# Node numbers for the one-hots kept in PSUM and counted on by VectorE from step ten

## The chip, the cores and the metric

One Trainium2 chip, one of its cores. The metric is the device time of one execution in microseconds, the median of three runs.

## What is computed

One layer of a graph network over 6250 nodes of width 256 with 100,000 edges that are sorted by their target node. A graph convolution (gather, sum by target node, divide by degree) and a linear attention are added to the input; then a mixture of eight experts of width 1024 with a capacity works on the result.

```python
Wh = x @ W + b                         # _L0_gnn_ref, on the normalized x
summed = jax.ops.segment_sum(Wh[edge_src], edge_dst, num_segments=N_NODES)
deg = jax.ops.segment_sum(jnp.ones(...), edge_dst, num_segments=N_NODES)
h = summed / jnp.maximum(deg, 1.0)[:, None]
...
x = x + _L0_gnn_ref(xn, W, b, src, dst) + _L0_mix_ref(xn[None], ...)[0]
x = x + _L0_ffn_ref(_layernorm(x)[None], ...)[0]     # top-1 of 8 experts, capacity 977
```

## The kernel before

The nodes are cut into 49 tiles of 128 (`NT`). The segment sum of a tile is a matmul on TensorE: for each chunk of 128 edges, a one-hot matrix (edges by nodes) times the gathered rows. A one-hot is made by VectorE: it compares the 128 node numbers of the tile with the target of each edge (`is_equal`). Chunks go in groups of four (`G`), and gathered groups stand in a ring of seven (`RQ`).

**GpSimd (POOL)** gathers. `gather` issues four indirect DMAs per group (L614), each of which takes 128 row numbers from `idx` in SBUF; 196 groups make 784 such DMAs. Before every even group it looks whether a tile's results are due (`events`): if group f lies more than `LAG` = 5 past the last group of tile t+2, `event(t)` waits until VectorE has placed tile t (`row_ok`), scatters its rows (L564) and, from tile ten on, sends the rows of one finished expert job (`finish`, L551). Then it goes on gathering.

**VectorE** runs one `step` per tile: `late` (one-hots beyond the first four groups, L1462), `degrees` (L1564 counts the degree from PSUM, then L1573 to L1576), `early` for the next tile (L1488, four groups in one instruction of 128 x 2048), `combine`, `node_out`, `place` (ends with `row_at`, L1649, and `row_ok`), `plan`, `residual`, `route`, and `post` of an expert job. **TensorE** in a step does the projection of the last tile, one expert job (`expert`, `hidden`), the transposes, and then the sum of the next tile. **ScalarE** scales the sum (`ready`), normalizes a job's rows, takes a square root (`deviation`, L764), and does the hidden layer's ReLU (L799). SyncE loads weights and rows.

Steps 0 to 9 carry the attention (`pairs`); there the early one-hots are made in four parts (`early_part`). Steps from `T0` = 10 on carry expert jobs. After step 48 there are no sums left and the remaining expert jobs run.

The node numbers stand in `node_ids`, an SBUF tile of two halves: tile t uses half t % 2. In every step ScalarE adds 256 to the half of tile t (`count_on`, L732) behind `ready`, so that it serves tile t + 2, and VectorE waits for that (`nodes_ok`) inside `degrees`, behind L1564. `one_hot` and `early` read `node_ids` and `dst_t`, both in SBUF. The bank `pQ` holds the attention's queries up to step nine and nothing later.

## Time and profile before

| | us |
|---|---|
| median of three runs | 1847.22 |
| lowest, highest | 1834.12, 1854.69 |
| span of the profiled execution | 1845.7 |
| device time of the profiled execution | 1847.46 |
| POOL busy | 962.5 |
| PE busy | 1258.2 |
| VectorE busy | 860.2 |
| ScalarE busy | 556.7 |

The profile shows one execution. Busy time of POOL is that of its DMA-building and copy instructions; its register and semaphore instructions don't count. An instruction's row has its start, its length, and in brackets how long its engine had been idle before it and what released it; "issue" means that the profile shows no release. Short VectorE instructions overlap a little, so the distance of two starts can be less than the length of the first.

### The profile page before, as it was taken

How to read it: one execution, taken by the hardware profiler on the slowest of the kernel's cores; microseconds unless marked ns; L12 is line 12 of the kernel's file. 1: busy time of each engine (PE TensorE's matmuls, PEld its weight loads, DVE VectorE, ACT ScalarE, POOL GpSimd, SP SyncE). 2: the span in 40 equal slices, each digit the busy share in tenths (PEclk: the TensorE clock that was granted, in tenths of full speed). 3: DMA queues.
4: the chain of work that ended last, by engine and by line, in shares of the span. 5: the costliest groups of instructions: out<-in, count | busy, mean ns of one | idle time of the engine just before them, and what ended most of it. 6: DMA issues, size and time to landing. Idle time of an engine off the chain costs nothing.

```text
span 1845.7 us, 33822 instructions
## 1 busy us (share of the span) xinstructions
PE 1258.2 (68%) x5962; PEld 831.4 (45%) x5963; DVE 860.2 (47%) x3202; ACT 556.7 (30%) x1460; POOL 962.5 (52%) x969
## 2 busy tenths in 40 slices
PE   3767765453755776666567677767768678688696
PEld 2544444140422443333344444444446456466586
DVE  6723322121412433334345455556557567577554
ACT  5611112020211222122223233333434334344442
POOL 5556662626254443343756766666566666661111
PEclk8688886766967866666878788888889889899898
DMA  7752332323232332332444444444455454453363
GB/s 242 204 171 83 87 90 63 89 80 89 81 107 66 93 101 88 89 97 82 133 134 144 127 132 143 143 144 145 137 142 164 140 168 141 143 161 115 115 186 104
DMA packets 141741, 229.00 MB, mean 124 GB/s; under 512 B 29855, under 2 KB 86723, under 8 KB 141618
## 3 DMA queue, kind: packets, MB, share of 16 engines
q0 software_dynamic: 42800, 115.65, 21.0%
q1 hardware_dynamic: 97454, 111.65, 19.9%
q14 instruction: 104, 0.85, 0.2%
q10 hardware_dynamic: 1364, 0.54, 0.1%
q8 instruction: 19, 0.31, 0.1%
HBM read 194.65 MB, written 34.81 MB: 124 GB/s over the span
## 4 chain that ended last, share of the span: by engine, by line
PE 48%; issue 27%; DVE 8%; another core or an unknown queue 8%; ACT 2%; DVEq 2%; DMA 1%; POOL 1%; SPq 0%; ACTq 0%; POOLq 0%
PE pA L971 12%; PE pH L1126 8%; PE pY L1117 8%; PE pQ L1037 3%; PE pX L1094 3%; PE pD L974 3%; PE pH L948 2%; PE pY L1066 2%; PE pY L1064 2%; PE pH L1047 1%; POOL shared L614 1%; PE pH L1055 1%; PE pA L998 1%; DMA shared<-in_L_ffn_b_dram 1%
## 5 line engine op out<-in xcount | busy, mean ns | idle before, releaser
L614 POOL DMA_INDIRECT shared<-table,idx x784 | 812.7, 1037 | 553.3 <-issue 280.3
L971 PE MATMUL pA<-shared,onehot 128*128 x976 | 327.1, 452 | 287.6 <-issue 266.5
L971 PEld LDWEIGHTS pA<-shared,onehot 128*128 x976 | 102.9, 105 | 496.9 <-issue 455.0
L1126 PE MATMUL pH<-shared 128*128 128x128 f32 x1664 | 202.7, 277 | 25.7 <-issue 25.6
L1117 PE MATMUL pY<-w2s,shared 128*128 x832 | 201.2, 396 | 16.0 <-issue 12.4
L1126 PEld LDWEIGHTS pH<-shared 128*128 128x128 f32 x1664 | 197.9, 193 | 28.9 <-issue 26.1
L799 ACT ACTIVATE shared<-pH,b1s 128x128 f32<-128x128 f32 x416 | 116.5, 375 | 259.3 <-remote 216.5
L1117 PEld LDWEIGHTS pY<-w2s,shared 128*128 128x128 f32 x832 | 159.4, 197 | 41.6 <-issue 20.8
L727 ACT ACTIVATE shared<-pA,rdeg 128x256 f32<-128x256 f32 x49 | 23.3, 475 | 393.6 <-issue 212.2
L551 POOL DMA_INDIRECT out_dram<-shared,jtok x52 | 51.7, 994 | 158.2 <-issue 158.2
L1564 DVE CUSTOM_DVE_ANT_1 pD<-pD,ident 128x512 f32<-128x512 f32 x49 | 34.3, 700 | 201.1 <-issue 104.3
L564 POOL DMA_INDIRECT rows<-rows_sb,row_at x49 | 50.8, 1036 | 131.8 <-issue 131.8
L974 PE MATMUL pD<-onehot,c 128*128 x244 | 108.7, 445 | 8.4 <-issue 7.9
L737 ACT ACTIVATE shared<-pQ,bqs 128x128 f32<-128x128 f32 x196 | 60.4, 359 | 160.7 <-PE pQ L1037 92.7
L1677 DVE SCALAR_TENSOR_TENSOR shared<-pY,shared 128x256 f32<-128x256 f32 x52 | 25.2, 484 | 155.7 <-ACT shared L785 140.1
L1094 PE MATMUL pX<-wgs,shared 128*128 128x264 f32 x196 | 73.7, 511 | 29.4 <-issue 29.4
L1488 DVE TENSOR_TENSOR onehot<-node_ids,dst_t 128x2048 f16 (+1 forms) x39 | 89.5, 2296 | 9.0 <-issue 9.0
L948 PE MATMUL pH<-shared,w2s 128*128 128x257 f32 (+1 forms) x196 | 59.9, 433 | 48.8 <-issue 27.9
L1037 PE MATMUL pQ<-xts,wqs 128*128 (+1 forms) x392 | 75.2, 350 | 18.1 <-issue 12.3
L1037 PEld LDWEIGHTS pQ<-xts,wqs 128*128 128x128 f32 x392 | 65.1, 250 | 28.2 <-issue 28.0
L1462 DVE TENSOR_TENSOR onehot<-node_ids,dst_t 128x512 f32 (+1 forms) x65 | 45.0, 693 | 58.6 <-PE pD L974 31.9
L948 PEld LDWEIGHTS pH<-shared,w2s 128*128 128x128 f32 (+1 forms) x196 | 40.0, 212 | 62.4 <-issue 30.8
(278 smaller groups left out, 1875.0 us busy)
## 6 DMA issues: line engine op xcount, KB each, us to landing
shared<-in_L_ffn_w_dram SPq DMA_DIRECT2D x104, 512.0 KB
shared<-table,idx POOLq DMA_INDIRECT x784
w2s<-in_L_ffn_w_dram SPq DMA_DIRECT2D x8, 1024.0 KB, 5.8
rows<-rows_sb SPq DMA_DIRECT2D x7, 1040.0 KB
shared<-rows SPq DMA_DIRECT2D x52, 130.0 KB
shared<-in_L_ffn_b_dram SPq DMA_DIRECT2D x52, 128.0 KB
shared<-in_x_dram SPq DMA_DIRECT2D x12, 512.0 KB, 9.0
table<-w2s SPq DMA_DIRECT2D x12, 512.0 KB, 3.5
```

Of the source, the lines that this page charges most:

```text
L551: g.indirect_dma_start(out[:, :], bass.IndirectOffsetOnAxis(ap=jtok[:, b:b + 1], axis=0), fin[:, b, :], None, bounds_check=N - 1, oob_is_e ...
L614: g.indirect_dma_start(gathered[:, s * G + j, :], None, table[:, :], bass.IndirectOffsetOnAxis(ap=idx[:, q * G + j:q * G + j + 1], axis=0) ...
L737: ins = a.activation(out_[:, k * P:(k + 1) * P], pQ[:, k * P:(k + 1) * P], f, bias=bqs[:, k:k + 1])
L799: ins = a.activation(hs[:, h * FC // 2 + c, :], ph[:, c * P:(c + 1) * P], ACT.Relu, bias=b1s[:, bass.ds(e * FC + h * FC // 2 + c, 1)])
L948: ins = pe.matmul(gp[k][:, 0:DX], kr[0:rows_n, b, k * P:(k + 1) * P], xall[0:rows_n, t, :], start=False, stop=last)
L971: m = pe.matmul(pA[:, :], onehot[:, n % OQ, j, :], groups[:, f % RQ, j, :], start=False, stop=stop)
L974: m = pe.matmul(pD[:, :], ones16, onehot[:, n % OQ, :, :].rearrange("p g n -> p (g n)"), start=False, stop=False)
L1037: ins = pe.matmul(pQ[:, m * P:(m + 1) * P], wqs[:, k, m * P:(m + 1) * P], xts[:, bass.ds(t, 1), k, :].rearrange("p t n -> p (t n)"), start ...
L1094: ins = pe.matmul(pX[:, 0:GW], st[:, m * P:(m + 1) * P], wgs[:, m, :], start=(m == 0), stop=(m == DK - 1))
L1117: ins = pe.matmul(pY[:, 0:D], hs[:, c, :], w2s[:, bass.ds(e * FC * D + c * D, D)], start=(c == 0), stop=(c == FC - 1))
L1126: ins = pe.matmul((pH0, pH1)[h][:, c * P:(c + 1) * P], w1b[:, h, k, c * P:(c + 1) * P], xjt[:, k * P:(k + 1) * P], start=(k == 0), stop=(k ...
L1488: v.tensor_tensor(onehot[:, :, :, :].rearrange("p q g n -> p (q g) n"), nodes_of(t).rearrange("p (a n) -> p a n", a=1).broadcast_to([P, EA ...
```

## The change

From step ten on the node numbers stand in PSUM (`late_nodes`, 128 columns of `pQ`). VectorE itself adds 128 to them once a step, in `degrees`, right behind L1564; the first such addition (step ten) reads `node_ids`. `early` and the late one-hots of these steps read `late_nodes` for node numbers and `dst_t` in SBUF as before. ScalarE's `count_on` is left only in steps 0 to 8. VectorE no longer waits for `nodes_ok` from step ten on; it waits for its own addition (`ids_on`) before `early`.

```diff
+        late_nodes = pQ[:, 0:P]
...
-                if inner or t + 2 < NT:
+                if pairs and (inner or t + 2 <= T0):
                     count_on(t)
...
-                def early(t):
+                def early(nodes):
                     ch = v.snap(first_r)
                     v.tensor_tensor(onehot[:, :, :, :].rearrange("p q g n -> p (q g) n"),
-                                    nodes_of(t).rearrange("p (a n) -> p a n", a=1).broadcast_to([P, EARLY * G, P]),
+                                    nodes.rearrange("p (a n) -> p a n", a=1).broadcast_to([P, EARLY * G, P]),
...
                 def next_tile(t):
-                    early(t + 1)
+                    v.wait_ge(S["ids_on"], t - T0 + 1)
+                    hold(v, "dve_hold")
+                    early(late_nodes)
...
-                def degrees(t, more):
+                def degrees(t, more, counted):
...
                     if more:
                         v.reg_add(used_r, used_r, size_r)
                         take_ends()
-                        if not isinstance(t, int) or t > 0:
+                        if not counted:
+                            first = isinstance(t, int) and t == T0
+                            v.tensor_scalar(late_nodes, nodes_of(T0) if first else late_nodes, float(P), None, ALU.add).then_inc(S["ids_on"], 1)
+                        elif not isinstance(t, int) or t > 0:
                             v.wait_ge(S["nodes_ok"], t)
                             hold(v, "dve_hold")
...
-                        late(t)
-                        degrees(t, inner or t + 1 < NT)
+                        late(nodes_of(t) if pairs or not inner and t == T0 else late_nodes)
+                        degrees(t, inner or t + 1 < NT, pairs)
```

## Rows read from the trace of the kernel before

**Rows 1.** The page, costliest groups: name, count, busy us, mean ns, idle before.
```profile
L614 POOL DMA_INDIRECT shared<-table,idx x784 | 812.7, 1037 | 553.3 <-issue 280.3
L1488 DVE TENSOR_TENSOR onehot<-node_ids,dst_t 128x2048 f16 (+1 forms) x39 | 89.5, 2296 | 9.0 <-issue 9.0
```

**Rows 2.** Windows: the gathering phase of the expert steps, and the end.
```profile
core 0: us, PE busy (x) PEld busy (x) DVE busy (x) ACT busy (x) POOL busy (x), PEclk, DMA share, GB/s
882.00:1664.00 782.00, 570.57 (x2911) 379.70 (x2910) 450.28 (x1669) 277.68 (x679) 510.44 (x480) 0.85 0.47 143
1704.00:1846.00 142.00, 110.75 (x714) 99.79 (x712) 73.02 (x326) 56.38 (x166) 18.72 (x19) 0.91 0.44 132
```

**Rows 3.** Windows of three steps: short, long, and one without gathers.
```profile
1192.30:1209.40 17.10, 14.59 (x88) 10.28 (x86) 12.66 (x48) 7.77 (x19) 11.04 (x11) 0.99 0.49 138
1209.40:1239.10 29.70, 18.51 (x93) 11.60 (x91) 12.72 (x47) 7.78 (x19) 19.75 (x20) 0.77 0.49 147
1671.30:1687.30 16.00, 13.16 (x79) 9.55 (x78) 12.26 (x47) 7.77 (x19) 2.29 (x3) 1.00 0.34 112
```

**Rows 4.** Lines of POOL from 882 to 1664 us, and L1564 from 880 to 1710.
```profile
L614 POOL DMA_INDIRECT shared<-table,idx x398 | 435.0, 1093 | 185.2 <-issue 161.3 <-PE pA L971 23.5 <-DMA shared<-table,idx 0.5
L1564 DVE CUSTOM_DVE_ANT_1 pD<-pD,ident x39: 699/700/700, 882.2 to 1703.0; 128x512 f32<-128x512 f32 x39
```

**Rows 5.** Timeline of VectorE in the short step.
```profile
1192.32 0.70 DVE L1564 CUSTOM_DVE_ANT_1 pD<-pD,ident 128x512 f32<-128x512 f32 x1 [0.53 <-issue]
1193.11 0.15 DVE L1573 TENSOR_SCALAR small<-small 128x1 f32<-128x1 f32 x1
1193.69 2.29 DVE L1488 TENSOR_TENSOR onehot<-node_ids,dst_t 128x2048 f16 x1 [0.17 <-issue]
...
1196.30 0.41 DVE L1608 TENSOR_TENSOR rows_sb<-pX,shared 128x256 f32 x1
1196.63 0.16 DVE L1609 TENSOR_TENSOR lg<-pX,tg 128x8 f32<-128x8 f32 x1
...
1199.31 0.16 DVE L1649 SCALAR_TENSOR_TENSOR row_at<-sc 128x1 f32 x1
```

**Rows 6.** Timeline of POOL in the same step.
```profile
1193.49 0.95 POOL L614 DMA_INDIRECT shared<-table,idx  x1 [0.31 <-issue]
1194.75 2.06 POOL L614 DMA_INDIRECT shared<-table,idx  x1 [0.30 <-issue]
1197.11 0.95 POOL L614 DMA_INDIRECT shared<-table,idx  x1 [0.30 <-issue]
...
1203.29 1.02 POOL L564 DMA_INDIRECT rows<-rows_sb,row_at  x1 [1.47 <-issue]
```

**Rows 7.** Timeline: gathers beside VectorE instructions with one and with two SBUF tensors.
```profile
1239.12 0.70 DVE L1564 CUSTOM_DVE_ANT_1 pD<-pD,ident 128x512 f32<-128x512 f32 x1 [0.53 <-issue]
1239.27 0.95 POOL L614 DMA_INDIRECT shared<-table,idx  x1 [0.31 <-issue]
...
1219.17 0.48 DVE L1593 SCALAR_TENSOR_TENSOR shared<-shared,small,xts 128x256 f32<-128x256 f32 x1
1219.27 1.20 POOL L614 DMA_INDIRECT shared<-table,idx  x1 [0.30 <-issue]
```

**Rows 8.** Lines of VectorE, forms kept apart.
```profile
L1690 DVE TENSOR_TENSOR shared<-shared 128x256 f32 x49 | 20.8, 425 | 0.0
L1608 DVE TENSOR_TENSOR rows_sb<-pX,shared 128x256 f32 x44 | 18.3, 416 | 6.2 <-issue 5.3 <-remote 0.9
```

**Rows 9.** Timeline of ScalarE in the short step.
```profile
1194.02 0.39 ACT L732 ACTIVATE node_ids<-node_ids,eps  x1
...
1197.65 0.29 ACT L764 ACTIVATE small<-sc,eps 128x1 f32<-128x1 f32 x1 [1.44 <-DVE sc L1615]
```

**Rows 10.** Timeline of the long step: TensorE's sums, then POOL's last DMAs.
```profile
1219.01 0.38 PE L974 MATMUL pD<-onehot,c 128*128 x1
1222.82 0.38 PE L971 MATMUL pA<-shared,onehot 128*128 x1 [3.44 <-issue]
...
1232.70 1.87 PE L971 MATMUL pA<-shared,onehot 128*128 x4 [6.46 <-issue]
...
1229.55 1.03 POOL L564 DMA_INDIRECT rows<-rows_sb,row_at  x1 [0.30 <-issue]
1233.87 1.00 POOL L551 DMA_INDIRECT out_dram<-shared,jtok  x1 [3.30 <-issue]
```

**Rows 11.** Timeline of VectorE and POOL where POOL waits for the placing.
```profile
1513.32 0.16 DVE L1649 SCALAR_TENSOR_TENSOR row_at<-sc 128x1 f32 x1
...
1515.08 1.02 POOL L564 DMA_INDIRECT rows<-rows_sb,row_at  x1 [1.75 <-issue]
```

More of the change, by code:

```diff
@@ L247, in gps_block @@
           row_stored row_free scat_done plan_ok tail_ok w1a_in w1b_in b2_in b2_ok j_in xj_ok h0_ps h1_ps h_sb y_ps y_sb
-          fin_ok fin_sc fin_free dve_c agg_c share_c x1_c tb_c route_c place_c plan_c post_c nodes_ok sp_hold act_hold dve_hold
+          fin_ok fin_sc fin_free dve_c agg_c share_c x1_c tb_c route_c place_c plan_c post_c nodes_ok ids_on sp_hold act_hold dve_hold
           pool_hold pe_hold""".split()
@@ L1455, in _, with one_hot @@
                 v.reg_mov(used_r, 0)
-                def one_hot(ch, t):
+                def one_hot(ch, nodes):
                     g = v.snap(ch - v.snap(first_r))
@@ L1462, in one_hot @@
                     v.tensor_tensor(onehot[:, g % OQ, :, :],
-                                    nodes_of(t).rearrange("p (a n) -> p a n", a=1).broadcast_to([P, G, P]),
+                                    nodes.rearrange("p (a n) -> p a n", a=1).broadcast_to([P, G, P]),
                                     dst_t[:, bass.ds(ch % EQ * G, G)].rearrange("p (g a) -> p g a", a=1).broadcast_to([P, G, P]),
@@ L1466, in one_hot, with one_hots @@
                     v.reg_add(pair_r, pair_r, 1)
-                def one_hots(lo, hi, t):
+                def one_hots(lo, hi, nodes):
                     with v.Fori(lo, hi) as ch:
-                        one_hot(ch, t)
+                        one_hot(ch, nodes)
                 def load_ends(t):
@@ L1506, in some, with late @@
                     with v.If(mid < end):
-                        one_hot(mid, 0)
+                        one_hot(mid, nodes_of(0))
                         v.reg_add(mid_r, mid_r, 1)
                         v.sem_inc(S["dve_hold"], 1)
-                def late(t):
+                def late(nodes):
                     mid, end = v.snap(mid_r), v.snap(end_r)
                     with v.If(mid < end):
-                        one_hots(mid, end, t)
+                        one_hots(mid, end, nodes)
                         v.sem_inc(S["dve_hold"], 1)
                 def next_tile(t):
-                    early(t + 1)
+                    v.wait_ge(S["ids_on"], t - T0 + 1)
+                    hold(v, "dve_hold")
+                    early(late_nodes)
                     if not isinstance(t, int) or t + 2 < NT:
@@ L1757, in _ @@
                             take_ends()
-                            early(0)
+                            early(nodes_of(0))
                         if t - 2 in TICKS[1:]:
```

## The prediction

> **What bounds the kernel now.** I read the page first. POOL is busy for half the span, mostly with 784 gathers at a mean of 1037 ns [rows 1]; the change touches the steps that L1488 serves. The windows give the stage: from 882 to 1664 us POOL is busy for 510 of 782 us, and from 1704 to the end there are no gathers and no one-hots [rows 2]. So 142 us of the end can't change through this edit, nor can the 882 us ahead, where the old code stays. What can change is a stretch of 821 us, the 38 steps between the first and the last L1564 [rows 4].
>
> Steps come in two kinds. By the starts of L1564, 13 of the 38 last 25 us or more (368 us together) and 25 last less (452 us, 18.1 on average); three steps stand as windows [rows 3]. The step without gathers takes 16.0 us: that is what VectorE, TensorE and ScalarE need among themselves. The short one takes 17.1 with POOL busy for 11, the long one 29.7 with POOL busy for 19.75.
>
> Is POOL the bound? Its busy time leaves out 0.30 us between two gathers [rows 6] and the branches around L564 and L551. Its idle time in front of gathers is 185 us, of which only 24 are put down to a wait for TensorE or a landing [rows 4]; 398 x 0.30 = 119 of the rest is the fixed gap. In the long step POOL runs from gather to gather without a wait up to L564 at 1229.55, and TensorE goes on with its sums only afterwards [rows 10]. In the short step VectorE has placed the tile at 1199.31 + 0.16 and POOL comes to scatter it only at 1203.29 [rows 5, 6]. Where POOL comes late to its own event, it is the bound; where it must wait for L1649 [rows 11], it is not. I find POOL late, by 1 to 13 us, in most steps, and just in time or early in four. So POOL bounds most of this stretch, but the 16.0 us of the other engines are close behind.
>
> **What in POOL goes away.** A gather takes 0.95 us. The one that starts 1.06 us into L1488 takes 2.06 [rows 5, 6]: L1488 ends at 1195.98, and 1.23 us of it were left, 0.12 more than the stretch of 1.11. The gather ahead, at 1193.49, had started before L1488 and isn't stretched. Going through the timeline from 882 us on, I find 34 gathers stretched by an L1488, by 0.94 to 2.11 us, 47.1 us together, each by what was left of the one-hot less 0.12; and three by late one-hots (L1462), 1.1 us. L1593, whose two tensors also lie in SBUF, does the same on its scale: 1.20 instead of 0.95 [rows 7].
>
> Does a PSUM operand end it? L1564 reads `pD` in PSUM and `ident` in SBUF. A gather that starts 0.15 us into it, with 0.55 us left, takes 0.95 [rows 7]; I find 16 such from 882 us on, all between 0.94 and 0.98. The new one-hot has the same kinds of operands: PSUM and SBUF. So I count the 48.2 us as gone from POOL, 48.2 / 36 = 1.3 us per step with gathers.
>
> The Trainium skill (SBUF — State Buffer, "Who interferes with whom") says that a VectorE instruction with two SBUF inputs holds up a GpSimd instruction that reads SBUF; but it adds, as inferred, that `tensor_tensor` leaves descriptor generation alone. By the second sentence nothing would be released here and the time would stay; the stretched gathers contradict it, and the first sentence holds.
>
> **What is added.** (a) The count-on in VectorE: 38 instructions of 128 columns, PSUM to PSUM, in front of the path to `rdeg`. The trace has none of this form. Nearest row: L1608 reads PSUM for 256 columns, and the next starts 0.33 us after it [rows 5]; L1488 has 1792 columns more and takes 1.88 us more, 1.05 ns a column, so 128 columns less are 0.13 less: 0.20 us, an estimate. Bounds: 0 (it starts in the shadow of L1564's tail) and 0.33. (b) The wait on `ids_on` with its hold now stands in front of `early`, where VectorE's queue is short: the gap there is 0.17 us already [rows 5]; I add 0.1 (0 to 0.2). Behind it wait the one-hot, `combine` and everything up to `row_at`; for these wait TensorE's transpose of the sum and POOL's event. The old wait on `nodes_ok` lay under L1564's 0.70 us and returns nothing. Together 0.3 us per step, 38 x 0.3 = 11 us on VectorE, at most 38 x 0.53 = 20.
>
> (c) One-hots from PSUM: `tensor_tensor` over 256 columns takes 416 ns from PSUM and SBUF and 425 from SBUF alone [rows 8]: I change nothing for L1488's 2.29. The Trainium skill (VectorE: DVE Perf Modes, "The TRN2 errata") puts a fixed term of 120 cycles on a PSUM source against 58 on SBUF; by it 43 one-hots would cost 43 x 0.065 = 2.8 us more in sum. The rows show no such difference.
>
> (d) ScalarE loses 38 instructions of 0.39 us. Behind the one at 1194.02 it still waits 1.44 us for VectorE before L764 [rows 9]. That idle time hides it: no gain. Bank `pQ` has no other user in these steps.
>
> **The sum.** Long steps: POOL's run of 16 gathers sets the end, and VectorE's 0.3 us lie in its wait: 13 x 1.25 = 16 us less. Short steps with gathers, 22: each falls by up to 1.25 us, but not below 16.0 + 0.3 = 16.3; with their own lengths this gives 20 us less (15 fall in full or nearly, the rest stand at 16.0 to 17.4 already). The last three and the first: 4 x 0.3 = 1 us more. In all -35 us. POOL's event can't run ahead of `row_at` [rows 11], which moves 0.3 us later in its step; for that I take 2 us back: -33. The profiled execution has 1847.46 us of device time (span 1845.7), the median of the runs is 1847.22: 1814 either way.
>
> **The rivals.**
> *The saving is given back (0.29).* In the long step TensorE's next sum comes 3.44 us and the one after 6.46 us late by "issue" alone, with gathers present; it resumes 2 us after POOL's L564 has started, and POOL's own L551 comes 3.30 us late [rows 10]. Something slows all engines about 11 us into a long row of gathers and lets go about when it ends. If it goes by the gathers' density, the pause from the one-hot was relief, and denser gathers make it set in earlier; the 16 us of the long steps are then lost, and in the short ones half. -10, and -10 + 5 from VectorE: 1842. For it: such slow spells are nearly the whole difference between long and short steps. Against: the spell ends with the run, and the run ends earlier.
> *VectorE becomes the bound everywhere (within the forecast's upper end).* If (a) and (b) cost 0.53 us, the floor is 16.5: 5 us less gain, 1819.
> *Slower (0.08).* Runs of eight gathers now end just ahead of the slow spell, at 10.8 to 13 us; with a pause of 1.1 us inside. If without it the spell set in by gather six or seven, some of the 22 short steps would turn long, at 29.7 - 17.1 = 12.6 us each [rows 3]. Against a gain of 33 it decides from the third on; five such steps give 1847 - 33 + 63 = 1877.
> *The change doesn't do what it says (0.05).* The gathers stay stretched because `dst_t` still comes from SBUF as second operand. Against it stands L1564, whose second operand comes from SBUF too [rows 7]. Then only the 0.3 us remain, where VectorE binds, some 25 steps: 1847 + 7 = 1854.
>
> **How the numbers follow.** Forecast 0.58: 1814; its own range is 1799 (all 48 us come through) to 1828. Given back 0.29: 1828 to 1850. No effect 0.05, slower 0.08. The range 1798 to 1852 leaves out the slower case and a little beside it. One per cent is 18 us, about what a measurement of this kernel can tell from no change: faster by more than that is the forecast and a small part of the rival, 0.61; within it 0.32; slower 0.07.
>
> **What will show it.** Right: no gather beside L1488 over 1.0 us (before: 2.06); mean of L614 between step ten and the last gather 0.96 to 0.98 instead of 1.093; L1488 still at 2.29; from L1564 to L1488 1.6 to 1.7 us instead of 1.37; the stretch between first and last L1564 about 788 us instead of 821; long steps at 28, short ones at 16.3 to 17. Wrong: L614 at 0.95 but the stretch at 815 (given back; then long steps still near 28 to 30 and more "issue" on TensorE); L614 still over 1.05 (no effect); more than 13 steps over 25 us (slower).

## The result, and the profile after

The change made the kernel slower: 1906.6 us (median of four runs, 1885.83 to 1910.04) against 1849.8 for the kernel before (1834.12 to 1854.69), a ratio of 1.029 [1.025, 1.034]. The forecast was 1814. The profiled execution has a span of 1908.3 us, before 1845.7. The experiments met other chips, and this ratio belongs to one kind of them: where the kernel before takes 1484 us, the same change made it 1.6% faster. Below, a chip on which the kernel before takes about 1480 us is called quick, one on which it takes 1850 to 1873 us slow. First the trace of the first chip, a slow one.

Grouped lines of the kernel after, from 889 to 1766 us (name, count, busy us, mean ns, idle before it and its releasers); they answer to [rows 4] and to L1488 in [rows 1]:

```profile
L616 POOL DMA_INDIRECT shared<-table,idx x399 | 383.2, 960 | 195.5 <-issue 126.5 <-PE pA L973 69.0
L1128 PE MATMUL pH<-shared 128*128 128x128 f32 x1216 | 176.5, 299 | 120.3 <-issue 119.9
L1119 PE MATMUL pY<-w2s,shared 128*128 x601 | 162.0, 415 | 48.6 <-issue 47.3
L973 PE MATMUL pA<-shared,onehot 128*128 x563 | 152.1, 392 | 77.0 <-issue 70.4 <-POOLq L593 4.1 <-DVE onehot L1464 1.9
L1490 DVE TENSOR_TENSOR onehot<-pQ,dst_t 128x2048 f16<-128x2048 f32 x38 | 87.1, 2292 | 7.4 <-issue 7.3
L566 POOL DMA_INDIRECT rows<-rows_sb,row_at x38 | 38.8, 1022 | 161.1 <-issue 161.1
...
L1568 DVE CUSTOM_DVE_ANT_1 pD<-pD,ident 128x512 f32<-128x512 f32 x38 | 26.6, 700 | 75.9 <-PE pD L979 42.9 <-issue 33.0
L1575 DVE TENSOR_SCALAR pQ<-pQ 128x128 f32<-128x128 f32 x37 | 12.3, 332 | 0.0
```

The same view of the kernel before, from 882 to 1703 us, for the lines that stand in none of the groups above:

```profile
L971 PE MATMUL pA<-shared,onehot 128*128 x560 | 185.5, 449 | 159.8 <-issue 154.7 <-DVE onehot L1462 4.5
L1126 PE MATMUL pH<-shared 128*128 128x128 f32 x1216 | 150.1, 277 | 25.7 <-issue 25.6
L1117 PE MATMUL pY<-w2s,shared 128*128 x603 | 144.4, 393 | 4.0 <-issue 4.0
L564 POOL DMA_INDIRECT rows<-rows_sb,row_at x38 | 39.7, 1044 | 50.5 <-issue 50.5
L1564 DVE CUSTOM_DVE_ANT_1 pD<-pD,ident 128x512 f32<-128x512 f32 x38 | 26.6, 700 | 39.7 <-issue 31.3 <-PE pD L977 8.4
```

All later line numbers are two to seven higher than before: L616 is the gather (L614), L566 the scatter (L564), L973 the sum's matmul (L971), L1128 and L1119 the expert's matmuls (L1126, L1117), L1568 the degree count (L1564), L1490 the early one-hot (L1488).

Three things stand in these lines. First, the gathers are free: their mean is 960 ns instead of 1093 [rows 4], 51.8 us less in sum, and the one-hot still takes 2.29 us. Second, POOL does not turn this into time: in front of the scatter L566 it now idles for 161.1 us instead of 50.5. It spends 110.6 us more in waiting there than it did, twice what it saved. Counted in the traces, the scatter followed the end of the placing within 1.2 to 1.9 us, 1.2 being the least of all, in 14 of the 38 steps before and in 27 after: there POOL stood ready or came just in time. Third, TensorE: before its expert matmuls it idles for 120.3 + 48.6 = 168.9 us instead of 25.7 + 4.0 = 29.7, while before the sum's matmul it idles for 77.0 instead of 159.8. Over the three lines the idle time went from 189.5 to 245.9 us, 56.4 more, and VectorE's degree count now waits 42.9 us for TensorE instead of 8.4.

TensorE's clock isn't what costs: its granted mean over the stretch is 0.87 (below), and 0.86 from 882.2 to 1703 us of the kernel before, with 607 and 603 us of TensorE busy.

Degree counts of the kernel after (duration, first and last start), and the windows of its stretch and its end ([rows 4] and [rows 2]):

```profile
L1568 DVE CUSTOM_DVE_ANT_1 pD<-pD,ident x49: 699/700/700, 297.3 to 1766.3; 128x512 f32<-128x512 f32 x49
```

```profile
core 0: us, PE busy (x) PEld busy (x) DVE busy (x) ACT busy (x) POOL busy (x), PEclk, DMA share, GB/s
889.90:1766.30 876.40, 606.74 (x3096) 418.67 (x3095) 473.29 (x1821) 288.90 (x683) 460.20 (x486) 0.87 0.45 133
1766.30:1908.00 141.70, 110.63 (x719) 100.25 (x718) 74.02 (x329) 56.34 (x166) 18.67 (x19) 0.92 0.43 132
```

Step ten starts at 889.9 us instead of 882.2; no instruction up to there reads the new node numbers. On the second slow chip that part differs more: 898.1 and 896.5 us in two kernels with free gathers (a1, e6 below) against 882.8 in e2r, which runs the same instructions up to there. Whether that is more than what one execution differs from another is not shown. The end is 142 us as before. The stretch between took 876.4 us instead of 820.8: 55.6 more, nearly all of the loss. By steps, the 13 of 25 us or more grew from 368 to 411 us (one of them from 28.2 to 47.8, while the one behind it fell from 23.8 to 17.2), the 25 others from 452 to 465.

A short step of the kernel after, 18.0 us from 1698.5: TensorE, then POOL, then VectorE.

```profile
1699.32 3.72 PE L1119 MATMUL pY<-w2s,shared 128*128 x16 [0.17 <-issue]
1702.87 2.17 PE L1128 MATMUL pH<-shared 128*128 128x128 f32 x18
1706.00 0.27 PE L1128 MATMUL pH<-shared 128*128 128x128 f32 x1 [0.96 <-issue]
1706.74 1.70 PE L1128 MATMUL pH<-shared 128*128 128x128 f32 x13 [0.47 <-issue]
```

```profile
1695.29 0.99 POOL L616 DMA_INDIRECT shared<-table,idx  x1 [1.41 <-issue]
...
1700.35 0.95 POOL L616 DMA_INDIRECT shared<-table,idx  x1 [0.30 <-issue]
1701.60 0.94 POOL L616 DMA_INDIRECT shared<-table,idx  x1 [0.30 <-issue]
...
1704.10 0.95 POOL L616 DMA_INDIRECT shared<-table,idx  x1 [0.30 <-issue]
1708.88 1.02 POOL L566 DMA_INDIRECT rows<-rows_sb,row_at  x1 [3.83 <-issue]
```

```profile
1699.13 0.33 DVE L1575 TENSOR_SCALAR pQ<-pQ 128x128 f32<-128x128 f32 x1
...
1699.97 2.29 DVE L1490 TENSOR_TENSOR onehot<-pQ,dst_t 128x2048 f16<-128x2048 f32 x1 [0.20 <-issue]
...
1705.34 0.16 DVE L1651 TENSOR_REDUCE sc<-lg 128x1 f32<-128x8 f32 x1 [0.56 <-DVE lg L1650]
1706.71 0.17 DVE L1652 TENSOR_TENSOR cnt<-cnt,oh 128x8 f16<-128x8 f16 x1 [1.21 <-issue]
...
1707.47 0.16 DVE L1656 SCALAR_TENSOR_TENSOR row_at<-sc 128x1 f32 x1
```

And the same tile's step in the kernel before, 16.0 us from 1639.1: TensorE, then POOL, then VectorE's placing.

```profile
1637.06 3.70 PE L1117 MATMUL pY<-w2s,shared 128*128 x16
1640.60 3.73 PE L1126 MATMUL pH<-shared 128*128 128x128 f32 x32
```

```profile
1634.67 0.99 POOL L614 DMA_INDIRECT shared<-table,idx  x1 [2.67 <-issue]
...
1641.00 2.63 POOL L614 DMA_INDIRECT shared<-table,idx  x1 [0.30 <-issue]
...
1645.19 0.95 POOL L614 DMA_INDIRECT shared<-table,idx  x1 [0.30 <-issue]
1647.54 1.02 POOL L564 DMA_INDIRECT rows<-rows_sb,row_at  x1 [1.40 <-issue]
```

```profile
1646.13 0.16 DVE L1649 SCALAR_TENSOR_TENSOR row_at<-sc 128x1 f32 x1
```

Before, one gather of the eight is held for 2.63 us, the 32 expert matmuls run in 3.73 us without a gap, and POOL comes to the scatter after 1.40 us of idling: the placing (L1649) ends 0.15 us behind the last gather, so a shorter queue would have gained nothing in this step. After, no gather is held and the run of eight goes through in 9.8 us; but towards its end TensorE stops twice among the same 32 matmuls (0.96 and 0.47 us by "issue"), VectorE idles for 1.21 us between L1651 and L1652, its placing (L1656) comes 9.0 us after the degree count at 1698.52 (the median of before is 7.0), and POOL, which must wait for the placing, idles for 3.83 us. These are the slow spells that the prediction spoke of. In them register and semaphore instructions of TensorE, VectorE, SyncE and GpSimd, whose medians are 51, 40, 34 and 34 ns in this stretch, take about 0.7 us each: here one of TensorE at 1700.99 took 707 ns and one of VectorE at 1703.85 took 683. ScalarE has none.

### The profile page after: what moved, and what is told of

Read it like the earlier page. It is cut to its first block, busy times and chain, and to the rows that moved or that the text cites. A ratio compares the mean times of both kernels' runs of the same rounds, so it can differ in the third digit from the quotient of the medians.

```text
span 1908.3 us, 33781 instructions
## 1 busy us (share of the span) xinstructions
PE 1264.8 (66%) x5962; PEld 849.6 (45%) x5963; DVE 854.5 (45%) x3240; ACT 549.9 (29%) x1422; POOL 904.4 (47%) x969
## 4 chain that ended last, share of the span: by engine, by line
PE 43%; issue 31%; DVE 9%; another core or an unknown queue 6%; DVEq 3%; ACT 3%; POOL 2%; DMA 1%; SPq 0%; ACTq 0%; POOLq 0%
PE pA L973 9%; PE pH L1128 8%; PE pY L1119 8%; PE pQ L1039 3%; PE pX L1096 2%; POOL shared L616 2%; PE pH L950 2%; PE pY L1068 2%; PE pD L976 2%; PE pY L1066 2%; PE pH L1049 1%; PE pH L1057 1%; DMA shared<-in_L_ffn_b_dram 1%; DVEq L1477 1%
## 5 line engine op out<-in xcount | busy, mean ns | idle before, releaser
L616 POOL DMA_INDIRECT shared<-table,idx x784 | 758.4, 967 | 567.3 <-PE pA L973 275.8
L973 PE MATMUL pA<-shared,onehot 128*128 x976 | 294.4, 420 | 227.3 <-issue 196.9
L1128 PE MATMUL pH<-shared 128*128 128x128 f32 x1664 | 229.1, 292 | 120.3 <-issue 119.9
L973 PEld LDWEIGHTS pA<-shared,onehot 128*128 x976 | 98.9, 101 | 416.6 <-issue 371.8
L1128 PEld LDWEIGHTS pH<-shared 128*128 128x128 f32 x1664 | 219.4, 207 | 131.6 <-issue 128.2
L1119 PE MATMUL pY<-w2s,shared 128*128 x832 | 218.4, 411 | 60.9 <-issue 56.1
L1119 PEld LDWEIGHTS pY<-w2s,shared 128*128 128x128 f32 x832 | 159.7, 201 | 102.7 <-issue 82.7
L566 POOL DMA_INDIRECT rows<-rows_sb,row_at x49 | 49.9, 1019 | 247.9 <-issue 247.9
L1568 DVE CUSTOM_DVE_ANT_1 pD<-pD,ident 128x512 f32<-128x512 f32 x49 | 34.3, 700 | 261.1 <-PE pD L979 180.2
L976 PE MATMUL pD<-onehot,c 128*128 x244 | 101.1, 414 | 8.1 <-issue 7.9
L1490 DVE TENSOR_TENSOR onehot<-pQ,dst_t 128x2048 f16<-128x2048 f32 x38 | 87.1, 2292 | 7.4 <-issue 7.3
L1096 PE MATMUL pX<-wgs,shared 128*128 128x264 f32 x196 | 65.6, 464 | 37.1 <-issue 34.9
L704 ACT ACTIVATE w2s<-w2s 128x256 f32<-128x256 f32 x49 | 20.4, 416 | 154.5 <-DVE w2s L1443 81.3
```

The source lines that it names most:

```text
L616: g.indirect_dma_start(gathered[:, s * G + j, :], None, table[:, :], bass.IndirectOffsetOnAxis(ap=idx[:, q * G + j:q * G + j + 1], axis=0) ...
L973: m = pe.matmul(pA[:, :], onehot[:, n % OQ, j, :], groups[:, f % RQ, j, :], start=False, stop=stop)
L976: m = pe.matmul(pD[:, :], ones16, onehot[:, n % OQ, :, :].rearrange("p g n -> p (g n)"), start=False, stop=False)
L1096: ins = pe.matmul(pX[:, 0:GW], st[:, m * P:(m + 1) * P], wgs[:, m, :], start=(m == 0), stop=(m == DK - 1))
L1119: ins = pe.matmul(pY[:, 0:D], hs[:, c, :], w2s[:, bass.ds(e * FC * D + c * D, D)], start=(c == 0), stop=(c == FC - 1))
L1128: ins = pe.matmul((pH0, pH1)[h][:, c * P:(c + 1) * P], w1b[:, h, k, c * P:(c + 1) * P], xjt[:, k * P:(k + 1) * P], start=(k == 0), stop=(k ...
```

## The experiments

Theories named in the expectations: *pace* (the hold was a rest for the gathers that put the slow spells off), *spell* (the loss comes through the slow spells alone), *VectorE* (the counting-on and its wait lengthen each step), *GpSimd bound* (whatever lengthens or shortens POOL's queue arrives in the time).

**Pause, counting-on alone, lighter traffic.** The first four kernels ran on a chip on which the kernel before takes 1480.1 us instead of 1850.

e1: the changed kernel with a pause in POOL before every second group, 91 times two memsets of 0.427 us (77.7 us). With their waits they lengthen the break between two gathers from 0.30 to 1.27 us, which puts 88 us into POOL's queue.

```diff
+                if q % 2 == 1 and not first:
+                    for k in range(2):
+                        g.wait_ge(S["rested"], i * 14 + ((q - 1) // 2) * 2 + k)
+                        hold(g, "pool_hold")
+                        g.memset(rest_t[:, :], 0.0).then_inc(S["rested"], 1)
                 for j in range(G):
                     g.indirect_dma_start(gathered...
```

> The changed kernel, with two small POOL memsets (128 x 384 fp16, about 1.1 us together with their waits) after every fourth gather of each eight, in all steps. They write only and read nothing in SBUF. Pace theory (the one-hot's hold on a gather was a rest that put off the slow spells): 1840 to 1865 us, short steps back under 17.5 us, first slow sequencer row later in a run than in the changed kernel. VectorE theory (the addition and its wait lengthen each step): the pause brings nothing, 1905 to 1940 us.

Measured: 1514.6 us, ratio to the kernel before 1.024 [1.021, 1.026].

e2: VectorE counts on, but in SBUF; the one-hots read two SBUF tensors again, and gathers are held as before.

```diff
-        late_nodes = pQ[:, 0:P]
+        late_nodes = node_ids[:, 0, :]
```

> The changed kernel with the counted node numbers left in SBUF: VectorE counts on and waits as in the change, but one-hots again read two SBUF tensors and hold a gather up. Pace theory: 1845 to 1865 us (before plus 0.3 us of VectorE in some steps). VectorE theory: 1890 to 1910 us, as the changed kernel.

Measured: 1480.6 us, ratio 1.001 [0.998, 1.005].

e3: the pause of e1 in the kernel before.

> The kernel before with the same pause of about 1.1 us after every fourth gather of each eight. Pace theory, if more rest is worth more than it costs: 1800 to 1840 us, the slow spells of the runs of sixteen gathers shorter than 13 us. If a rest is worth only what the gathers lose by it, or less: 1850 to 1880 us.

Measured: 1549.2 us, ratio 1.048 [1.045, 1.051].

e4: the changed kernel with the w1 loads after the first job cut from 512 columns to 32, so that hidden layers are computed with old weights.

```diff
-                    sp.dma_start(w1b[:, h, :, :], w1_v[..., h * 512:h * 512 + 512]...
+                    c1 = 512 if first else 32
+                    sp.dma_start(w1b[:, h, :, 0:c1], w1_v[..., h * 512:h * 512 + c1]...
```

> The changed kernel with each load of the first expert weights cut from 512 to 32 columns after the first job (so the output of later jobs is not the reference's); it takes about 0.94 MB per step off SyncE's queue. Traffic theory (the slow spells come from gathers and weight loads together): spells after step ten mostly gone, 1740 to 1800 us. Pace theory without traffic: spells as before, 1890 to 1910 us.

Measured: 1432.1 us, ratio 0.967 [0.965, 0.970].

What follows: counting on by VectorE costs nothing that can be measured (e2). The traces of this chip have not one register or semaphore instruction between 0.55 and 1.5 us on TensorE, VectorE or GpSimd from step ten to the last sum; register loads from memory (VectorE has one of 0.55 us or more in every step, in every trace) and DMA-issuing instructions are left out of this and of all counts below. With no slow spells to break, a pause can only cost, so e1 and e3 do not test the pace theory here, nor e4 the traffic theory (beside a2's 0.984 below, its 0.967 only says that the bytes of these loads are worth some 26 us without slow spells); and the changed kernel itself had not run on such a chip.

**The changed kernel, its counting-on, and the one-hot's source, on a slow chip.** Here the kernel before takes 1873.4 us. a1 is the changed kernel as it is.

> The changed kernel itself, unaltered, beside the kernel before. On the chip of the first measurement both kernels had stretches in which every sequencer instruction of VectorE, TensorE, SyncE and GpSimd took about 0.7 us; on the chip of the first experiments neither kernel had any. Spell theory: the loss of 2.9% comes through those stretches (steps after ten with longer pieces of them), so on a chip without them the changed kernel is within 1% of the kernel before or a little faster, ratio 0.985 to 1.005. VectorE theory: the loss is VectorE's own extra chain (numbers counted on and waited for ahead of each tile's one-hot, 0.3 us a step, 28 steps, and all that queues behind it), which needs no slow stretch, so the ratio is 1.01 to 1.03 on any chip.

Measured: 1918.1 us, ratio 1.023 [1.017, 1.028]. The profiled execution (1933.8 us) is 0.8% above that median; those of the first chip and of e6, read beside it below, are not above theirs by more than 0.2%.

e6: the counting-on moved ahead of the wait for TensorE's last product.

```diff
                     k = part("agg_c", t)
+                    if more and not counted:
+                        ...                       # waits: oh_late, oh_ready (not in the first)
+                        v.tensor_scalar(late_nodes, ..., float(P), None, ALU.add).then_inc(S["ids_on"], 1)
                     v.wait_ge(S["agg_done"], t + 1)
```

> The changed kernel with VectorE's counting-on moved ahead of its wait for TensorE's last aggregation product, so that it runs while VectorE would idle; the one-hots still read PSUM. VectorE theory: the chain from TensorE's last product to the next tile's one-hot gets back to the length of before (1.37 us instead of 1.6), so the kernel gains about 0.25 us on each of 28 steps, ratio to the changed kernel 0.995 or lower. Spell theory and pace theory: no difference to the changed kernel that can be measured (within 0.3%).

Measured: 1933.8 us, ratio 1.033 [1.027, 1.039]. From the degree count to the one-hot it takes 1.39 us (median of 38 steps) where the changed kernel takes 1.45 and the kernel before 1.38, and yet it is no faster; it is 15.7 us slower than a1, where the spell and pace theories expected no difference. Nothing here explains that.

e2r: e2 again, VectorE's numbers in SBUF.

> VectorE counts on as in the changed kernel, but the one-hots from step ten on compare with node numbers in SBUF, so that two-operand reads from SBUF are back and hold up the gathers as before. Against the changed kernel this shows what the PSUM source alone does: if freeing the gathers is worth the 48 us of GpSimd time, this kernel is 2% slower than the changed one; if freeing them is given back or harmful, it is level with it (within 0.5%) or faster. Against the kernel before it shows the counting-on alone: 11 us or 0.6% at most by the step costs, and 0.1% by the first run of it.

Measured: 1869.1 us, ratio 1.001 [0.998, 1.004].

This settles which part does it. The VectorE theory falls: with the counting-on kept and the numbers in SBUF the kernel is level with before on both kinds of chip, and with the chain shortened and PSUM kept it is not better. On the slow chip the whole loss comes with the PSUM source. That it comes through the gathers set free is an inference: of what else a PSUM source could change, the one-hot's length stayed (2292 ns) and the addition's place in the chain was ruled out by e6; no run here has the PSUM source and held gathers. The same grouped lines of e2r, from 882.8 to 1716.1 us, where gathers are held:

```profile
L973 PE MATMUL pA<-shared,onehot 128*128 x560 | 183.9, 450 | 128.2 <-issue 126.7 <-POOLq L593 0.8
L1128 PE MATMUL pH<-shared 128*128 128x128 f32 x1216 | 158.2, 282 | 49.6 <-issue 49.6
L1119 PE MATMUL pY<-w2s,shared 128*128 x602 | 148.8, 402 | 16.6 <-issue 16.4
L566 POOL DMA_INDIRECT rows<-rows_sb,row_at x38 | 39.2, 1033 | 60.7 <-issue 60.7
```

and of a1, from 898 to 1786.3 us, where they are free:

```profile
L1119 PE MATMUL pY<-w2s,shared 128*128 x603 | 171.7, 430 | 62.3 <-issue 61.5
L1128 PE MATMUL pH<-shared 128*128 128x128 f32 x1216 | 169.8, 292 | 116.7 <-issue 116.5
L973 PE MATMUL pA<-shared,onehot 128*128 x560 | 150.8, 392 | 71.2 <-issue 65.5 <-POOLq L593 3.4 <-DVE onehot L1464 2.0
L566 POOL DMA_INDIRECT rows<-rows_sb,row_at x38 | 38.9, 1024 | 181.3 <-issue 181.3
```

The picture of the first chip again: idle time before the three TensorE lines 194.4 against 250.2 us (55.8 more), the stretches 833.3 and 888.2 (54.9 more), and 60.7 against 181.3 us before the scatter. Medians on that chip: 1869.1 and 1918.1, 49.0 us apart. Where the slow spells fall I counted in the traces, from step ten to the last sum (slow: 0.55 to 1.5 us):

```
                                     before   e2r   | after   a1     e6
gathers held by one-hots               yes    yes   |   no     no     no
runs of 8 or 9 gathers                 22     20    |   25     25     26
  without any slow instruction          5      5    |    1      1      1
slow instr., TensorE and VectorE      205    209    |  220    216    233
slow instr., GpSimd                    68     60    |   29     26     26
first slow one, us into a run of 8-9   11.8   10.3  |    7.1    7.2    6.5
the same, runs of 12 and more          12.7    9.8  |    6.8    7.2    5.8
degree count to placing, us             7.0    7.0  |    9.0    9.9    9.6
```

(The last three are medians over the runs that have a slow instruction of TensorE or VectorE; the first-slow row of "before" is over its 21 runs with a held gather. How many runs there are depends a little on the break that is taken to end one.) There are hardly more slow instructions. They come 3 to 5 us earlier in a run, and so they fall on VectorE's placing and TensorE's expert matmuls instead of behind them; the placing then comes 2 to 3 us later, and POOL, ready early, waits for it.

**The changed kernel on a quick chip.** Kernel before: 1484.3 us. a2 is the changed kernel as it is.

> The changed kernel again, as the measure for the three that follow on the same chip. On a chip where sequencer instructions of 0.7 us appear (kernel before near 1850 us) both theories expect 1.02 to 1.03 times the kernel before; on one where none appear (kernel before near 1480 us) the pace theory expects 0.97 to 0.99 and says that the freed GpSimd time then arrives, while a theory in which freed gathers hurt by themselves expects over 1.01 there too.

Measured: 1457.9 us, ratio 0.984 [0.980, 0.987]: 26 us faster. Here are the grouped lines of a2 from 626.5 to 1312.5 us:

```profile
L973 PE MATMUL pA<-shared,onehot 128*128 x560 | 153.4, 399 | 109.8 <-POOLq L593 54.7 <-issue 52.1 <-DVE onehot L1464 3.0
L1128 PE MATMUL pH<-shared 128*128 128x128 f32 x1216 | 145.7, 279 | 8.0 <-DMA shared<-in_L_ffn_w_dram 8.0
...
L566 POOL DMA_INDIRECT rows<-rows_sb,row_at x38 | 39.4, 1036 | 42.2 <-issue 36.9 <-DVEq L1658 5.1 <-DVE shared L1697 0.3
```

and the windows of that stretch in a2 and in e2, which is level with the kernel before and stands in for it on a quick chip:

```profile
626.50:1312.50 686.00, 555.41 (x3097) 393.61 (x3096) 476.17 (x1821) 289.98 (x683) 463.58 (x486) 0.95 0.54 170
```

```profile
625.70:1338.60 712.90, 562.57 (x3080) 399.45 (x3079) 480.23 (x1822) 289.44 (x683) 514.82 (x486) 0.93 0.52 164
```

51.2 us less of POOL give 26.9 us less of stretch; four steps of 25 us or more become two, and the short ones stay at a median of 16.3 to 16.4. TensorE waits for POOL's report of landed gathers (L593), as it should where POOL bounds. The placing comes 7.05 us after the degree count, as in the kernel before. This is the mechanism that was forecast, and the VectorE theory, which wanted 1.01 to 1.03 on any chip, falls once more.

p1 and p3 are e1 and e3 again, beside a2.

> The changed kernel with GpSimd writing a scratch buffer twice (0.43 us each) before every second group of four gathers, so that no run of gathers goes on for more than four without a pause; the one-hots still leave the gathers alone. Pace theory: where the slow sequencer instructions appear, what hurts the changed kernel is eight gathers in a row with no break, so the pause (78 us of GpSimd time in all) costs less than it saves: faster than the changed kernel by 1% or more, level with the kernel before, and next to no slow instructions in steps with eight gathers. Rival, GpSimd bound: the pause is only work in GpSimd's queue, and the kernel is 1 to 3% slower than the changed one, as its 1.024 against the kernel before on the other chip suggests.

Measured: 1515.7 us, ratio 1.022 [1.019, 1.026], 4.0% above a2 where the rival expected 1 to 3.

> The kernel before with the same pause. Pace theory, strong form (unbroken gathers alone bring the slow instructions): the steps before ten, whose gathers have no break either, get faster where slow instructions appear, so this one is faster than the kernel before, ratio under 0.99. Weak form (only the place of the pause beside each tile's end matters): ratio 1.00 to 1.02. GpSimd bound: 1.03 to 1.05, as on the other chip.

Measured: 1546.6 us, ratio 1.042 [1.038, 1.047].

The pause cost 57.7 us in the changed kernel and 62.3 in the kernel before: on a quick chip some two thirds of the 88 us that it puts into POOL's queue reach the end.

h1: gathers of half a row.

```diff
-                    g.indirect_dma_start(gathered[:, s * G + j, :], None, table[:, :],
+                    half = not (first and q < RQ)
+                    g.indirect_dma_start(gathered[:, s * G + j, 0:D] if half else gathered[:, s * G + j, :], None,
+                                         table.rearrange("n (h d) -> (n h) d", h=2) if half else table[:, :],
```

> The changed kernel with gathers that move 512 bytes for each node instead of 1024 (from the 29th gather on; the other half of each slot keeps old values, so the sums are not the reference's): as many gathers and descriptors, half the bytes. Bytes theory: if the slow sequencer instructions come from the traffic that the gathers make, they nearly go, and the kernel is faster than the changed one by 3% or more. Descriptor theory: they come from GpSimd's issuing of gathers, whose number stays, and the kernel is within 1% of the changed one and shows as many slow instructions.

Measured: 1443.6 us, ratio 0.973 [0.969, 0.977], 14 us below the changed kernel. Halving the bytes of the gathers is worth 1% where there are no slow spells; what it does to them this chip can't say.

**In search of a slow chip.** Pause and half rows had to be tried where slow spells appear. Three more chips were quick ones (kernel before 1480.0, 1481.1 and 1480.5 us). On the first, q1 is the changed kernel with the pause, q2 the one with half rows, q3 the kernel before with the pause; on the second r1 and r2, on the third s1 repeat q1 and q2.

> The changed kernel with GpSimd's pause (two memsets of 0.43 us) before every second group of gathers, meant for a chip on which the kernel before takes about 1850 us. There the changed kernel is at 1.023 to 1.029. Pace theory: what brings the slow sequencer instructions is eight gathers in a row with no break; with the pause the ratio to the kernel before is 1.00 to 1.015 and steps with eight gathers have fewer than 20 slow instructions in TensorE's and VectorE's queues together where the changed kernel has some 100 in the steps under 22 us. GpSimd bound: the pause adds its own cost as on the quick chips (1.022 to 1.024 there where the changed kernel was 0.984), so the ratio is 1.05 or more. If the kernel before comes at about 1480 us here, both expect 1.02 once more.

> The changed kernel with gathers of 512 bytes for each node instead of 1024, as many gathers and descriptors. Bytes theory: the slow sequencer instructions come from the bytes that the gathers move; the ratio to the kernel before falls to 0.99 or less where the changed kernel is at 1.023 or more, and slow instructions nearly go. Descriptor theory: they come from the issuing of gathers itself; the ratio stays at 1.01 or more and the slow instructions are as many. On a quick chip: 0.973, as measured.

> The kernel before with the same pause. Pace theory: the first ten steps, in which gathers run unbroken in both kernels, get faster by more than the pause costs there, so the ratio is at most 1.00. GpSimd bound: 1.04 or more, as on the quick chips.

> As before: on a chip where the kernel before takes about 1850 us, the pace theory expects the changed kernel with pauses at 1.00 to 1.015 times the kernel before, where the changed kernel is at 1.023 to 1.029; GpSimd bound expects 1.05 or more. At about 1480 us for the kernel before both expect 1.02.

> As before: with half the bytes in each gather, on a chip where the kernel before takes about 1850 us, the bytes theory expects 0.99 or less and hardly any slow sequencer instructions, the descriptor theory 1.01 or more and as many of them. At about 1480 us: 0.974.

> As before: on a chip where the kernel before takes about 1850 us, the pace theory expects the changed kernel with pauses at 1.00 to 1.015 times the kernel before; GpSimd bound expects 1.05 or more. At about 1480 us for the kernel before both expect 1.02.

Measured: the changed kernel with the pause 1.024, 1.019 and 1.021; with half rows 0.975 and 0.968; the kernel before with the pause 1.047. All as on the quick chips before; on the slow spells they say nothing.

g1: half the pause, one memset (91 x 0.43 = 39 us busy), on a slow chip (kernel before 1868.5 us).

> The changed kernel with one memset of 0.43 us (not two) on GpSimd before every second group of gathers: half the pause. On a chip where the kernel before takes about 1480 us, the changed kernel is at 0.984 and with the full pause at 1.019 to 1.024: if GpSimd's queue bounds throughout, the half pause stands in the middle, 1.000 to 1.005; if half of it fits into waits that GpSimd has anyway, it stays under 0.995. On a chip where the kernel before takes about 1850 us, the pace theory expects 1.00 to 1.015 (the changed kernel is at 1.023 to 1.029 there), GpSimd bound 1.04 or more.

Measured: 1914.5 us, ratio 1.025 [1.020, 1.030]. POOL around one pause, and its scatter from 897.3 to 1768.7 us:

```profile
1663.69 0.95 POOL L622 DMA_INDIRECT shared<-table,idx  x1 [0.30 <-issue]
1664.64 0.43 POOL L620 MEMSET rest_t<- 128x384 f16 x1
1665.23 0.95 POOL L622 DMA_INDIRECT shared<-table,idx  x1 [0.16 <-issue]
```

```profile
L567 POOL DMA_INDIRECT rows<-rows_sb,row_at x38 | 38.7, 1020 | 137.0 <-issue 137.0
```

The memset fills the gap that is there anyway: the break between the two gathers is 0.60 us instead of 0.30, so the pauses put 91 x 0.29 = 27 us into the queue and not 39. Both theories fall as they were put. GpSimd bound (1.04 or more): the ratio is that of the changed kernel on the two other slow chips, 1.023 and 1.029, and POOL's idle time before the scatter is 137.0 us where it was 181.3 (a1) and 161.1 (first chip), so the pauses fit into waits. The changed kernel wasn't measured on this chip, and by the intervals a cost of up to 1% can't be excluded. Pace theory (1.00 to 1.015): a break that is 0.3 us longer behind the fourth of eight gathers does not give the time back. Its first slow instruction comes at 6.5 us into a run, and the idle time before the expert matmuls is 161.3 us: a kernel with free gathers in every respect. A held gather lasts 0.94 to 2.11 us longer than a free one, three to seven times the 0.29 us added here; the full pause of e1 (0.97 us longer) was never run on a slow chip, so that a longer rest would help there is neither shown nor excluded.

## Why the prediction was wrong

The parts of the change were sized well: 51.8 us of gathers came free where 48.2 were counted (the sum then takes 1.25 us a step, a little under its own 48.2 / 36 = 1.34). Gathers that start inside the one-hot take 0.94 to 0.97 us; the mean of L616 is 960 ns, forecast 960 to 980; the one-hot takes 2292 ns from PSUM and took 2296 from SBUF. The counting-on was priced too high: with its wait it moved the one-hot from 1.38 to 1.45 us behind the degree count, 0.07 us a step instead of 0.3, and e2 and e2r find the whole of it at 1.001. "Doesn't do what it says" and "VectorE becomes the bound" fell with that. ScalarE brought nothing that could be seen.

**The Trainium skill** (SBUF — State Buffer, "Who interferes with whom") was weighed for the hold itself; with one operand in PSUM the hold is gone in every trace (66 gathers begun inside a one-hot of the kernel after, none over 0.97 us), so its rule on two SBUF inputs agrees, and its inferred exception for `tensor_tensor` doesn't. By the fixed term that the Trainium skill gives for a PSUM source (VectorE: DVE Perf Modes, "The TRN2 errata") L1490 would be some 65 ns longer than L1488, an estimate; the measured difference is -4 ns.

**The step that failed** is the sum's last one, that POOL's event can't run ahead of the placing, "for that I take 2 us back". It was sized as if the placing stayed where it was but for 0.3 us, and as if a freed run of gathers left the slow spells where they were. It measured 110.6 us of added idling before the scatter [rows 11 show one such wait of before, 1.75 us], because VectorE's placing itself moved by 2 us and more. The reading under it was off too: POOL was said to be just in time or early in four steps, and the trace of before has 14 of 38 in which the scatter follows the placing at the least distance (1.2 to 1.9 us); in these a shorter queue has nothing to give. That alone doesn't turn the sign: on the quick chip, with the same placing as before, about half of the freed time arrived. In the sum's terms: the long steps were to fall by 1.25 us each and rose by 3.3 (1.95 without the one of 47.8), the short ones were to fall by 0.9 and rose by 0.5.

**The rivals.** The onset was named in the rival "Slower": without the pause the slow spell may set in by gather six or seven. It did, at 6.5 to 7.2 us instead of 10 to 12. Its price was not what happened: on the first chip no short step turned long (13 steps of 25 us or more before and after; "more than 13" was to be its sign), and on the second only two, from 23.0 and 24.5 us in e2r to 26.6 and 29.7 in a1 (12 and 14 such steps); of the 25 short ones of the first chip 14 grew, by 0.5 to 3.6 us, and 7 fell. The expert matmuls paid, a place that the prediction never looked at although their idle time of 29.7 us in 821 showed how well they were placed. (The long step's row that "Given back" starts from is misread by a little: TensorE resumes 3.2 us after L564 has started, not 2 [rows 10].) "Given back" had the cause half right and assumed that relief and saving could at most cancel. Together these two had 0.37, but 0.07 for slower by over 1% looks far too little, in hindsight, for a trace in which slow spells made nearly the whole difference between long and short steps, and in which the thing removed was a break right ahead of them.

**A condition that nothing in the profile of before could show** is the chip. The same two kernels stand at 1.029, 1.023 (slow chips) and 0.984 (quick chip), so whether the direction came out right was also luck. On the quick chip the forecast's mechanism gave -26 us of the -33. What differs between the chips lies where gathers run: the ten first steps and the prologue took 626 us instead of 882, the stretch of kernels with held gathers 713 instead of 821 to 833, and the end without gathers is 142 to 146 us on both, at nearly the same granted clock (0.91 to 0.92 in before and e2r, 0.92 to 0.93 in a2 and e2). Each chip was met only once, so whether it is the chip itself or its state at that time is not shown. Nor is the part of the clock: up to step ten the granted mean is 0.74 on the slow chips and 0.90 to 0.91 on the quick ones, and TensorE is busy for 544 to 549 us instead of 464. These 80 to 85 us are the most that a lower clock can have added to TensorE's own work; the rest of the 256 us is idle time.

**Shown**: that the one-hot's PSUM source, which sets the gathers free, and not the counting-on, makes the loss on a slow chip (e2r, a1); that it goes with an earlier onset of the slow spells and with idle time in the expert matmuls and before the scatter; that without spells the freedom gains (a2). **Not shown**: what the slow instructions wait for, why only some chips have them, whether it is the hold as such that delayed them (no pause of its length ran on a slow chip), and where e6's further 0.8% comes from.

## What to carry to other kernels

A hold-up of an engine that is nearly the bound may be a break that others live on: before removing it, look at what comes right after it in time, and at which engine waits for whom once the freed one runs ahead. When an engine's instructions get shorter and its idle time grows by more, its queue does not bound the new kernel, and a small delay put into it (here 27 us without a cost that could be told) says so in one run, best beside the same kernel without it; first read from the trace how much the delay really adds. A difference of 2% that hangs on the timing of bursts should be measured on more than one chip; here its sign changed.

## What the runs showed of the hardware

- One kernel differs by a quarter between chips: the kernel before took 1850, 1873 and 1868 us in three measurements and 1480 to 1484 in five on five other chips, and the difference lies in the part with gathers (step ten is reached after 882 us instead of 626, and the stretch behind it takes 821 to 833 instead of 713).
- On the slow ones, and only there, register and semaphore instructions of about 0.7 us appear on four engines, from mostly 5 to 13 us into a run of gathers until mostly 1 to 4 us behind its last gather. Fewer of them were GpSimd's own when the gathers were free (68 and 60 against 26 to 29).
- A gather that begins inside a VectorE `tensor_tensor` of 128 x 2048 with both inputs in SBUF lasts 0.94 to 2.11 us longer than 0.95 us (34 in the kernel before); with one input in PSUM none of 66 lasts over 0.97 us.
- A VectorE `tensor_scalar` of 128 columns from PSUM to PSUM is recorded with 332 ns, but the one-hot behind it starts only 60 ns later than where the addition runs ahead of the degree count (1.45 us behind the count in a1, 1.39 in e6).
- A memset of 0.43 us between two gathers lengthens the break between them by only 0.29 us (0.60 instead of 0.30 us in g1), two of them by 0.97 us (e1).
